# A macaron layer of MoE, memory attention and MoE: token-stationary router products, a four-block first routing, and earlier weight splits

## What is computed

```python
x = x + 0.5 * ffn(layernorm(x), gate_w, w1, w2)      # first MoE
x = x + attn(layernorm(x), ...)                      # memory attention, not touched here
x = x + 0.5 * ffn(layernorm(x), gate_w, w1, w2)      # second MoE

def ffn(tokens, gate_w, w1, w2):                     # 8 experts, capacity 320
    probs = softmax(tokens @ gate_w)                 # [T, 8]
    expert = argmax(probs)                           # top 1
    mask = one_hot(expert, 8)
    pos = cumsum(mask, 0) - 1                        # place of a token in its expert
    sec = mask[:, :, None] * one_hot(pos, 320)       # tokens past 320 are dropped
    h = relu(gathered(sec, tokens) @ w1[e])          # 256 -> 1024
    y = h @ w2[e]                                    # 1024 -> 256
    return sum over e of probs * scattered(sec, y)
```

## Time and profile before

| what | us |
|---|---|
| median of 3 runs (lowest to highest) | 972.88 (970.96 to 977.67) |
| span of the profiled execution | 973.9 |
| first stage, start to the first routing operation | 0 to 50.4 |
| first routing, to its last index | 50.4 to 76.1 |
| from there to the first up product | 76.1 to 103.4 |
| pair 0 of the first MoE, to the first up product of pair 1 | 103.4 to 144.5 |
| attention, from the first MoE's end to the second routing | about 250 to 777 |
| second MoE: first routing operation, first up product, first up of pair 1 | 777.0, 826.7, 864.5 |

### The profile page before, as it was taken

One profiled execution on the slowest core, in us unless ns is written; L12 is line 12 of the kernel. 1 busy time (PEld: TensorE's weight loads), 2 busy tenths in 40 slices (PEclk: granted clock), 3 DMA queues, 4 the chain that ended last, 5 costly groups with the idle time before them and its releaser, 6 DMA issues. The chain is left out here.

```text
span 973.9 us, 15603 instructions
## 1 busy us (share of the span) xinstructions
PE 794.4 (82%) x5632; PEld 722.8 (74%) x5632; DVE 700.0 (72%) x1644; ACT 420.9 (43%) x837; POOL 245.6 (25%) x172
## 2 busy tenths in 40 slices
PE   5921989999266899999999999999877423999996
PEld 1311889999255788989888898989867412999996
DVE  0085759774558899999999998998832185877861
ACT  1202626542042738274573738365432103654650
POOL 0005432131101214060332414050321105423112
PEclk9955799999678999999999999999958555999999
DMA  5886842400310103012120303002020144545100
GB/s 186 301 302 181 256 162 99 152 27 15 100 43 1 44 2 115 16 60 71 44 86 0 129 0 96 33 0 86 1 87 1 50 166 146 184 128 176 54 23 28
DMA packets 58018, 88.91 MB, mean 91 GB/s; under 512 B 6705, under 2 KB 48881, under 8 KB 57841
## 3 DMA queue, kind: packets, MB, share of 16 engines
q1 hardware_dynamic: 46848, 70.44, 22.1%
q0 software_dynamic: 3840, 10.49, 3.3%
q10 hardware_dynamic: 7280, 7.34, 2.4%
HBM read 74.63 MB, written 22.02 MB: 99 GB/s over the span
## 5 line engine op out<-in xcount | busy, mean ns | idle before, releaser
L519 PE MATMUL ps<-weights_high_down,moe_hidden_high 128*128 128x256 f32 (+1 forms) x384 | 109.0, 284 | 2.6 <-DVE moe_rows L394 2.6
L521 PE MATMUL ps<-weights_high_down,moe_hidden_low 128*128 128x256 f32 (+1 forms) x384 | 107.9, 281 | 0.0
L520 PE MATMUL ps<-weights_low_down,moe_hidden_high 128*128 128x256 f32 (+1 forms) x384 | 107.9, 281 | 0.0
L519 PE MATMUL ps<-moe_normedT_high,weights_high_up 128*128 128x320 f32 x256 | 82.7, 323 | 2.1 <-DVE moe_hidden_low L386 1.0
L520 PE MATMUL ps<-moe_normedT_low,weights_high_up 128*128 128x320 f32 x256 | 80.7, 315 | 0.0
L521 PE MATMUL ps<-moe_normedT_high,weights_low_up 128*128 128x320 f32 x256 | 80.6, 315 | 0.0
L386 DVE SCALAR_TENSOR_TENSOR moe_hidden_low<-ps,moe_hidden_high 128x320 fp32r<-128x320 f32 x128 | 62.6, 489 | 21.1 <-ACT moe_hidden_high L481 18.3
L481 ACT ACTIVATE moe_hidden_high<-ps 128x320 fp32r<-128x320 f32 x128 | 56.2, 439 | 38.3 <-PE ps L521 25.5
L461 ACT CAST weights_high_up<-weights_raw_up 128x256 fp32r<-128x256 f32 x128 | 43.8, 404 | 64.1 <-PEq L104 64.1
L519 PEld LDWEIGHTS ps<-weights_high_down,moe_hidden_high 128*128 128x128 f32 (+1 forms) x384 | 69.3, 181 | 2.8 <-issue 2.8
L521 PEld LDWEIGHTS ps<-weights_high_down,moe_hidden_low 128*128 128x128 f32 (+1 forms) x384 | 69.4, 181 | 0.0
(11 more groups left out here) (240 smaller groups left out, 2346.4 us busy)
## 6 DMA issues: line engine op xcount, KB each, us to landing
weights_raw_up<-in_w SPq DMA_DIRECT2D x16, 1024.0 KB
weights_raw_down<-in_w SPq DMA_DIRECT2D x16, 1024.0 KB
xt<-in_xT SPq DMA_DIRECT2D x8, 1024.0 KB, 4.9
att_x_res<-x SPq DMA_DIRECT2D x8, 1024.0 KB, 5.5
out_x<-att_x_res SPq DMA_DIRECT2D x8, 1024.0 KB, 4.4
att_x_norm<-x ACTq DMA_DIRECT2D x7, 1024.0 KB, 5.4
att_x_norm<-x SPq DMA_DIRECT2D x1, 1024.0 KB, 5.4
att_GATE<-in_w_x SPq DMA_DIRECT2D x1, 704.0 KB
```

What stands on the lines that cost most here:

```text
L519: mm(dst, high_l, high_r, start=start, stop=False)
L520: mm(dst, high_l, low_r, start=False, stop=False)
L521: return mm(dst, low_l, high_r, start=False, stop=stop)
```

## The change

`first_logits` and the first use of `route` become one stage, `first_route`. In it 128 tokens of `xt` are the stationary operand and `gate_c` streams, so that logits come out with tokens on partitions. The routing goes in four blocks of 16 token tiles: VectorE's chain for a block runs while TensorE does the products of the next, with counts and table products between the product groups. GpSimd makes two of the three versions of `col_hot`. SyncE loads two small constants, then `xt` (eight buffers, four loads in flight) and the weights of pair 0; six constants go by ScalarE's queue. ScalarE makes the high parts of `UP[0]`, `UP[1]`, `DOWN[0]` of pair 0 and GpSimd the low part of `UP[0]` inside the routing stage, in both MoEs.

In `experts`, gathers have one semaphore per tile, and `norm` waits tile by tile. The copy `x1 <- x` is issued by SyncE after the gathers of pair 0, ahead of the attention's constants. The router logits of a pair move behind `up(g,0)`, those of VectorE's steps on them into the second eight. In pair 0 the low pieces of `UP[1]` and `DOWN[0]` go where `DOWN[1]` and `UP[0]` of pair 1 were; these two follow later.

```diff
+        @block.scalar
+        def _(act):
+            weights.first_high(act)
+
+        @block.gpsimd
+        def _(pool):
+            weights.first_low(pool)
...
+    def first_high(self, act):
+        for u in self.UNITS[0:3]:
+            act.wait_ge(self.loaded[u], 16)
+            for f in range(KF):
+                self.nc.scalar.copy(self.piece(self.high, u, f), self.piece(self.raw, u, f)
+                                    ).then_inc(self.high_done[u], 1)
+
+    def first_low(self, pool):
+        u = self.UNITS[0]
+        for f in range(KF):
+            pool.wait_ge(self.high_done[u], f + 1)
+            self.nc.gpsimd.tensor_tensor(self.piece(self.low, u, f), self.piece(self.raw, u, f),
+                                         self.piece(self.high, u, f).bitcast(F32),
+                                         ALU.subtract).then_inc(self.low_done[u], 1)
...
-            sp.wait_ge(gathered, 16 * PT)
+            for i in range(PT):
+                sp.wait_ge(gathered[i], 16 * (before + 1))
+            if x_copy is not None:
+                sp.dma_start(*x_copy).then_inc(copied, 16)
...
-                pool.wait_ge(gathered, 16 * PT * (g + 1))
-            if result_ready is not None:
-                pool.wait_ge(result_ready, 16)
+                for i in range(PT):
+                    pool.wait_ge(gathered[i], 16 * (before + g + 1))
+            if copied is not None:
+                pool.wait_ge(copied, 16)
...
-                dve.wait_ge(gathered, 16 * PT * (g + 1))
                 for i in range(PT):
+                    dve.wait_ge(gathered[i], 16 * (before + g + 1))
...
             def pair(g, first, last):
                 for f in range(KF):
                     low_hidden(g, 0, f)
+                    low_piece(g, UP[1] if first else DOWN[1], f)
+                for f in range(KF):
+                    low_hidden(g, 1, f)
                     if f == 0:
                         shifted_logits(g)
                     elif f == 3:
                         probability(g, first)
-                    low_piece(g, DOWN[1], f)
-                for f in range(KF):
-                    low_hidden(g, 1, f)
-                    if not last:
+                    if first:
+                        low_piece(g, DOWN[0], f)
+                    elif not last:
                         low_piece(g + 1, UP[0], f)
+                if first:
+                    for f in range(KF):
+                        low_piece(g, DOWN[1], f)
                 if not last:
                     norm(g + 1)
                 finish(g, 0, 0)
                 if not last:
                     normalise(g + 1, False)
                 finish(g, 0, 1)
+                if first:
+                    for f in range(KF):
+                        low_piece(g + 1, UP[0], f)
                 if not last:
                     for f in range(KF):
                         low_piece(g + 1, UP[1], f)
...
-            for u in (UP[0], UP[1]):
-                for f in range(KF):
-                    low_piece(0, u, f)
+            v.memset(hidden_high[1][:, :, 0:D].bitcast(F32), 0.0).then_inc(padded, 1)
+            v.memset(hidden_low[1][:, :, 0:D].bitcast(F32), 0.0).then_inc(padded, 1)
             norm(0)
             normalise(0, True)
-            v.memset(hidden_high[1][:, :, 0:D].bitcast(F32), 0.0).then_inc(padded, 1)
             for i in range(TURNS):
                 split_turned(0, i)
-            v.memset(hidden_low[1][:, :, 0:D].bitcast(F32), 0.0).then_inc(padded, 1)
-            for f in range(KF):
-                low_piece(0, DOWN[0], f)
             pair(0, True, False)
...
                 for f in range(KF):
                     relu(g, 0, f, first)
-                    if f == 2:
-                        exponentials(g)
                     high_piece(g, DOWN[1], f, first)
                 for f in range(KF):
                     relu(g, 1, f, first)
+                    if f == 2:
+                        exponentials(g)
                     if not last:
...
-            for u in (UP[0], UP[1]):
-                for f in range(KF):
-                    high_piece(0, u, f, True)
             for i in range(TURNS):
                 turned_tiles(0, i, True)
-            for f in range(KF):
-                high_piece(0, DOWN[0], f, True)
             pair(0, True, False)
...
             def pair(g, first, last):
                 up(g, 0, first)
+                logits(g, first)
                 up(g, 1, first)
                 for j in range(NY):
                     down(g, 0, j, first)
                     down(g, 1, j, first)
                     if not last:
                         turn(g + 1, j, False)
-                        if j:
-                            logits(g + 1, j - 1, False)
-                if not last:
-                    logits(g + 1, TURNS - 1, False).then_inc(logits_done, 1)
...
+    GROUP, BLOCK, FLIGHT = 8, 16, 4
+    GROUPS, BLOCKS = NT // GROUP, NT // BLOCK
+    xt = [sb(f"xt{i}", [P, KH, GROUP * P]) for i in range(GROUPS)]
...
+            def load(i):
+                if i >= FLIGHT:
+                    sp.wait_ge(loaded[i % FLIGHT], 16 * (i // FLIGHT))
+                sp.dma_start(xt[i][:], xT_dram[:, i * GROUP * P:(i + 1) * GROUP * P].rearrange("(k p) n -> p k n", p=P)
+                             ).then_inc(loaded[i % FLIGHT], 16)
+
+            sp.dma_start(t["gate_w"][:], t["d_gate_w"].rearrange("(k p) e -> p k e", p=P)).then_inc(gate_loaded, 16)
+            sp.dma_start(t["mean_w"][:], t["d_mean_w"]).then_inc(gate_loaded, 16)
+            for i in range(GROUPS - 1):
+                load(i)
+            weights.load(sp, 0, Weights.UNITS[0])
+            load(GROUPS - 1)
+            for u in Weights.UNITS[1:]:
+                weights.load(sp, 0, u)
...
+                act.dma_start(dst, src).then_inc(consts, 16)
+            weights.first_high(act)
...
+            def columns(q):
+                hot = col_hot[q % 2]
+                pool.wait_ge(col_hit, q + 1)
+                g.tensor_tensor(hot[:, :, 1, :], hot[:, :, 0, :],
+                                bc(t["iota"][:, q * BLOCK:(q + 1) * BLOCK].unsqueeze(2), [P, BLOCK, ST]),
+                                ALU.mult).then_inc(col_hot_ready, 1)
+                g.tensor_scalar(hot[:, :, 2, :], hot[:, :, 0, :], t["partition"][:, 0:1], None,
+                                ALU.mult).then_inc(col_hot_ready, 1)
+
+            pool.wait_ge(consts, 16 * len(loads))
+            for q in range(BLOCKS - 1):
+                columns(q)
+            weights.first_low(pool)
+            columns(BLOCKS - 1)
...
+            def block_of(q):
+                c, lg, (cum, tot) = LINKS * q, logits_of(q), counts_of(q)
+                dve.wait_ge(made, 2 * q + 2)
+                v.tensor_reduce(top[:], lg, AX.X, ALU.max).then_inc(chain, 1)
...
+                v.tensor_tensor(col_hot[q % 2][:, :, 0, :], bc(col[:].unsqueeze(2), [P, BLOCK, ST]),
+                                bc(t["iota"][:, 0:ST].unsqueeze(1), [P, BLOCK, ST]), ALU.is_equal).then_inc(col_hit, 1)
+                for n in range(BLOCK):
+                    v.tensor_scalar(row_hot[q % 2][:, n, :], iota_bf[:], row[:, n:n + 1], None,
+                                    ALU.is_equal).then_inc(row_hot_ready, 1)
...
+            def products(i):
+                pe.wait_ge(loaded[i % FLIGHT], 16 * (i // FLIGHT) + 16)
+                for j in range(GROUP):
+                    n = (i * GROUP + j) % BLOCK
+                    for k in range(KH):
+                        last = mm(logits_of(i * GROUP // BLOCK)[:, n, :], xt[i][:, k, j * P:(j + 1) * P],
+                                  t["gate_c"][:, k, :], start=(k == 0), stop=(k == KH - 1))
+                last.then_inc(made, 1)
...
+            products(0)
+            products(1)
+            for q in range(BLOCKS - 1):
+                products(2 * q + 2)
+                if q:
+                    table(q - 1)
+                counts(q)
+                products(2 * q + 3)
+            table(BLOCKS - 2)
+            counts(BLOCKS - 1)
+            table(BLOCKS - 1)
...
-        with ExitStack() as ctx:
-            first_logits(nc, first, ctx, ps[:], t, d["x"], d["xT"], x1)
         with ExitStack() as outer:
             weights = Weights(nc, outer, moe, t, "weights1")
             with ExitStack() as ctx:
-                route(nc, moe, ctx, ps[:], t, "route1", weights)
+                first_route(nc, first, moe, ctx, ps[:], t, d["xT"], weights)
+            rows = "(a b) h -> a (b h)"
             with ExitStack() as ctx:
-                experts(nc, moe, ctx, ps[:], t, "moe1", weights, d["x"], x1, first["x_copied"], given)
+                experts(nc, moe, ctx, ps[:], t, "moe1", weights, d["x"], x1,
+                        (x1.rearrange(rows, a=P), d["x"].rearrange(rows, a=P)), first["x_copied"], given)
...
```

238 lines of the change are left out of this document (133 added, 105 removed).

## The result

| kernel | median us (lowest to highest) | ratio to the kernel before, 95% interval | profiled span |
|---|---|---|---|
| before, in the same comparison | 971.92 (969.65 to 977.67) | | 973.9 |
| changed | 1008.39 (1006.07 to 1010.96) | 1.036 [1.031, 1.041] | 1004.5 |

The account below looks back on a forecast made before the run. Bounds: TensorE in the MoE pairs, unoverlapped seams around the routing, DMA and TensorE sharing a loop at the start. 973.9 + 11.2 (copy, first MoE) + 0.7 (second MoE) = 985.8, median 1.0 below: 985 us, range 965 to 995.

Parts of the forecast that it names:

- the lock between GpSimd and VectorE: VectorE scans slowed by GpSimd's low pieces of UP[0] in the second MoE's routing: 0 to 4.8 us, 3 taken.
- later pairs keep their pace: MoE pairs after pair 1's first up product: they run on TensorE without slack, so no change there.
- Part 1: Router products of the first stage: 256 records at 0.218 us, lower clock, 55.8 us, last product ending at 65.7.
- Rival B: Clock rises under the first stage's products: they cost 31.2 us, all that follows comes 24.6 earlier, 960 us; chance 0.12.
- Part 2: Routing tail after the last product: 8.4 us, plus 2.1 to the first gather, which comes at 76.2 against 77.26.
- Part 6: Second MoE, no copy: saving before first up product against GpSimd's lock, logits inside up and added low pieces; sum +0.7 us.
- rival C: GpSimd's gathers wait longer behind the copy, or its lock costs the first routing's tail too: 995 us; chance 0.10.
- Part 3: First MoE, gathers to first up product: moved logits save 6.2, tile-wise statistics 1.4; first up at 91.7, 11.7 earlier.
- Part 4: Copy of x ahead of constants and pair 1's UP[0]: ScalarE and TensorE wait; pair 1 starts 11.2 us later, at 155.7.
- G: Moment when all five gathers of pair 0 are in, first MoE; forecast 84.7, when the copy is issued.
- Part 5: GpSimd's gather waits before power(1), first MoE: free at G + 50, needed at G + 55, hidden with 5 us to spare.
- A: Rival: the copy holds nothing up; GpSimd's gathers bound pair 0, pair 1 at 139, 968 us; chance 0.18.

## Why the prediction was right in direction and wrong in size

In the profiles the change costs 30.6 us, forecast 11.9. The steps that failed, in the prediction's own terms: the lock between GpSimd and VectorE, put at nothing in the first tail (4.4 us); the way from the copy to pair 1, 3.5 too short; "later pairs keep their pace", where each MoE has one more set of logits behind pair 1 (about 2.5); and the saving in front of the first up product, taken as if it were there in full at pair 1 of the second MoE (1.4 of it was not).

**Part 1, products: right.** 0.215 per record, end at 64.8. Rival B (clock rises) is refuted by the profile, and by the run with wide products between.

**Part 2, tail: 5.1 us short.** From the last product to the first gather 15.6 us, not 10.5; the products ended 0.9 early, so the first gather is 4.2 late. I let GpSimd do two column products per block and took the cover (part 1) for granted: the low pieces of `UP[0]` stand in GpSimd's program between `columns(2)` and `columns(3)`, and run beside VectorE's `row_hot` of block 2. Part 6 priced that very exclusion for the second MoE, and the first routing has it just the same; I had it only as half a sentence in rival C. First gather 80.4, not 76.2; without the low pieces on GpSimd 76.0. That this meets my 76.2 is luck in part: there the products end at 64.4, 1.3 before my figure, and the tail is 11.6. I left `row_hot` of the last block (3.4) out of it; the last table products wait for that, as the earlier trace rows had named it, and not for GpSimd's columns, which I counted.

**Part 3, gather to first up product: right.** 15.15 against 15.5. The split of it into 6.2 for the logits and 1.4 for the tile waits holds too (6.3 and 1.35 alone).

**Part 4, the copy: the mechanism right, the size short.** `UP[0]` landed at G + 43.5 (I had 42); the last hidden split came 8.3 later (7.5); and pair 1 began 22.7 behind it, where I had 21.5. That term failed in its last part: `finish(0,2)` came where I had it, but from its end to pair 1 lie 7.8 us and not 6.6. Added to the 3.9 that G was late, this gives 18.6 instead of 11.2. The 3.9 may be less in effect, since the run without GpSimd's low pieces brought pair 1 only 2.7 sooner.

**Part 5, GpSimd hidden: right in the first MoE, where power(1) followed VectorE, and left out for the second.** In the first the gathers were in at G + 53 (I had G + 50), with 4.4 us to spare (I had 5). But hidden is not free: the run with the copy behind `UP[1]` shows that, with the other delay cured, the gathers' wait alone makes pair 1 14.5 late, though the copy goes out 18 us later there and meets the gathers of pairs 2 and 3. In the second MoE a gather held power(1) by 1.65: the changed kernel reaches the first up product 7.95 sooner behind the first gather, and power(1) only 2.2 sooner (42.8 against 45.0). The 5.8 between went into the logits inside `up`, eight more low pieces, and 1.65 of waiting for a gather.

**Part 6, second MoE: +6.3 instead of +0.7.** The exclusion cost 4.2, near the upper bound of my range and not the 3 that I took; 0.5 more went by before the first gather. (In the earlier trace rows VectorE's operation ended 0.55 behind GpSimd's, and not with it as I read.) In the experts I added +2.4 for logits and +2.8 for low pieces and subtracted 7.6, as if what is saved before the first up product were saved at pair 1. Measured from first gather to pair 1: 59.9 against 60.9, -0.9, where my terms give -2.3. From pair 1 to the end come another +2.5 (111.8 against 109.4), where I had nothing: the later pairs did not keep their pace, since one set of logits more stands in them. Together +1.5. The moved logits, alone, cost 9.5 from the first up product on, not 2.4: one set of logits more, and the wait for the gathers in the place of the time saved.

**The sum.** 11.2 + 0.7 = 11.9 forecast. In the profiles 20.1 to the end of the first MoE (11.2 forecast; 7.4 of the difference stand at pair 1, 1.5 in the later pairs, where the moved logits alone add 2.5: 105.4 from pair 1 to the last scatter against 102.9), 4.2 in the attention (within what its clock varies by in one kernel), 6.3 in the second MoE: 30.6. The medians differ by 36, which the profiles don't show in full: the profiled execution of the kernel before has a span 2.0 above its median (973.9 against 971.92), that of the changed kernel one 3.9 below it (1004.5 against 1008.39).

**Rivals.** A was refuted: the copy holds what stands behind it. With the copy early pair 1 starts 53.0 behind the last statistics, the 54 that A gave. C named the exclusion in the first tail, which came, and GpSimd's wait behind the copy in the first MoE, which VectorE covered. It had 0.10 and 995 us.

## To carry to other kernels

A transfer of many microseconds is hidden by where it is issued, not by being needed late: here 8.4 MB behind the products held nothing up and the same behind the gathers cost 22 us at pair 1. It held two queues at once, its own and the gathers', and curing its own alone gave back only a third, because then the other ended last. Before a saving in front is booked, look for what else must be in by the next meeting point: here gathers bounded power(1), and moving 6 us of logits out of the way of the first up product lost 3 in all. Small pieces given to an idle engine are free only if a neighbour doesn't slow down beside them; look at what it does in that very stretch.

## What the runs showed of the hardware

- f32 products with 128 stationary columns and 8 streaming ones, with a few count and table products between, ran 57 us without a gap at the lower clock, 0.215 us a record. After it had risen under wide products, some 40 of them ran at the higher one (0.117), and the rest at the lower again.
- The clock column reads 1.00 from the start to the first recorded fall, at either level (here to 100 us, with 0.215 and 0.27 us spacings in it).
- The higher level in the attention's last 60 us is granted differently in two executions of the same kernel, worth 4.5 us (526.2 and 530.7); over all kernels 526 to 534.
- A VectorE operation of 0.18 us took 0.69 beside GpSimd's f32 pieces of 0.69, one for one.
- Beside an 8.4 MB copy of SyncE's queue, the five gathers of pair 1 kept GpSimd waiting 22.6 us, and 5.0 with the copy early. An issue in SyncE's queue behind that copy took 20.24 us instead of 0.47.
